# Routing stage of a two-layer kernel: key sums after the next chunk's second key tile, with keys kept in two buffers

## The reference, cut to what matters

```python
xn = _layernorm(x)
s = L1_attn(xn)          # linear attention
g = silu(L1_ffn(xn))     # 64 experts, top 6, and a shared expert
x = x + s * g

# of L1_attn, the part that the change touches
k = gelu(x @ Wk.T + bk) + 0.21
v = x @ Wv.T + bv
k_r = rope(k)
z = 1.0 / (einsum("bhnd,bhd->bhn", qh, kh.mean(axis=2)) + 1e-06)   # sum of k over a sequence
kv = einsum("bhnd,bhne->bhde", krh * scale, vh * scale)            # sum of k_r (x) v over a sequence
```

## Time and profile before

| what | value |
|---|---|
| time, median of 3 runs | 6141.93 us (6138.8 to 6146.82) |
| the profiled execution's own time | 6135.09 us |
| its span in the trace | 6133.2 us |
| busy share of the span | PE 85%, DVE 72%, ACT 46%, POOL 49% |
| granted TensorE clock, mean | 0.923 |

### The profile page before, as it was taken

The page is one execution under the profiler, slowest core; times in us unless marked ns, Lnnn a source line. Parts: engine busy times, 40 slices in busy tenths (PEclk is TensorE's granted clock), DMA queues, the critical chain, the costliest instruction groups (busy, mean ns, idle before and its releaser), DMA issues. The chain is left out here.

```text
span 6133.2 us, 79104 instructions
## 1 busy us (share of the span) xinstructions
PE 5235.2 (85%) x26286; PEld 3098.7 (51%) x26286; DVE 4390.5 (72%) x8723; ACT 2850.5 (46%) x6074; POOL 3005.0 (49%) x1603
## 2 busy tenths in 40 slices
PE   6777677676757999999899899999989988888877
PEld 2222222222214666666555566666655555556755
DVE  5999999999996777777333477777743347674249
ACT  5666666766653555555111255555521123332233
POOL 5989989989994444444111244444411100002724
PEclk8888888888868999999999999999999989999988
DMA  5555555554541111111211111111121143333655
GB/s 130 127 118 132 134 122 129 131 127 124 122 100 47 32 35 32 36 32 32 64 52 52 50 34 34 35 32 35 32 57 52 52 137 124 115 115 110 167 178 191
DMA packets 475672, 530.96 MB, mean 87 GB/s; under 512 B 56438, under 2 KB 377988, under 8 KB 471172
## 3 DMA queue, kind: packets, MB, share of 16 engines
q1 hardware_dynamic: 456132, 515.24, 30.9%
q10 hardware_dynamic: 6848, 8.67, 0.5%
q0 software_dynamic: 12288, 2.00, 0.3%
HBM read 395.83 MB, written 146.82 MB: 88 GB/s over the span
## 5 line engine op out<-in xcount | busy, mean ns | idle before, releaser
L607 POOL TENSOR_TENSOR db<-durep,brep 128x2048 f32<-128x2048 f32 x256 | 1160.6, 4534 | 165.9 <-DVE p_h L514 155.7
L1080 POOL TENSOR_TENSOR rn<-n,mhalf 128x16 f32<-128x16 f32 x128 | 374.9, 2929 | 1077.7 <-DVE n L1041 1077.7
L466 ACT ACTIVATE p_h<-dlrep,am 128x512 f32<-128x512 f32 x1024 | 704.1, 691 | 210.5 <-DVE hh L525 179.2
L321 PE MATMUL p_acc<-hh,fold 128*32 128x512 f32 x2048 | 351.1, 765 | 511.7 <-DVE hh L525 510.7
L514 DVE TENSOR_TENSOR_SCAN p_h<-p_h,hlast,db 128x512 f32<-128x512 f32 x576 | 717.4, 1276 | 0.0
L935 ACT ACTIVATE probT<-p_t 128x512 f32<-128x512 f32 x256 | 152.9, 597 | 817.0 <-PE p_t L852 817.0
L525 DVE TENSOR_TENSOR hh<-p_h,crep 128x512 f32<-128x512 f32 x768 | 515.0, 671 | 0.0
L797 PE MATMUL p_qk<-wqkv,hT 128*128 128x512 f32 x1024 | 485.9, 598 | 2.5 <-DVE rot_sin L1035 1.6
L1374 POOL TENSOR_TENSOR grstd<-grstd,mhalf 128x4 f32<-128x4 f32 x32 | 32.6, 1018 | 789.7 <-DVE grstd L1301 789.7
L865 PE MATMUL p_o<-probT,v 128*64 128x128 f32 x4096 | 405.7, 279 | 12.6 <-DVE probT L1018 7.3
L865 PEld LDWEIGHTS p_o<-probT,v 128*64 128x64 f32 x4096 | 343.9, 137 | 136.7 <-issue 98.1
(11 more groups left out here) (269 smaller groups left out, 11836.8 us busy)
## 6 DMA issues: line engine op xcount, KB each, us to landing
dlrep<-delta_rows SPq DMA_DIRECT2D x256, 256.0 KB
durep<-drive_rows SPq DMA_DIRECT2D x256, 256.0 KB
ew<-in_L_ffn_w SPq DMA_DIRECT2D x192, 176.0 KB
brep<-bc_rows SPq DMA_DIRECT2D x64, 256.0 KB
crep<-bc_rows SPq DMA_DIRECT2D x64, 256.0 KB
delta_rows<-dl SPq DMA_DIRECT2D x64, 256.0 KB
drive_rows<-du SPq DMA_DIRECT2D x64, 256.0 KB
hx<-stream SPq DMA_DIRECT2D x256, 64.0 KB
```

The costliest lines, as they stand in the source:

```text
L321: ins = pe.matmul(p_acc[32 * j:32 * j + 32, :], fold[:], hh[s % 2][:, j], start=False, stop=(g == NG - 1), skip_group_check=True)
L466: act.activation(p_h[:, (i % BANKS) * CH:(i % BANKS + 1) * CH], dlrep[use % 2][:, j], ACT.Exp, scale=am[:, q, j, g:g + 1]).then_inc(s_ex, 1)
L607: pool.tensor_tensor(out=db[s % 2][:], in0=durep[use % 2][:], in1=brep[c % 2][:, g:g + 1, :].to_broadcast([P, 4, CH]), op=ALU.mult).then_i ...
L1080: pool.tensor_tensor(out=rn[k][:], in0=n2[k][:], in1=mhalf[:], op=ALU.pow).then_inc(s_rn, 1)
```

## The change

TensorE's `key_sums(c - 1)` is moved from behind `gate_scores(c)` to behind `keys(c, 1)`. Since keys(c, 0) would now overwrite rks before the sums of chunk c - 1 have read it, rks gets a second buffer and chunks alternate between them. VectorE's wait for the sums in keys(c, 0) is for the chunk two before, and `rotate(c)`, which has still one tile kr, gets a wait for the sums of chunk c - 1. VectorE's reading of a finished batch is moved from behind shared(c, 0) to behind normalise(c + 1), since the bank is complete only then. No instruction of work is added or removed.

```diff
-    ks = sb("rks", [P, CT, 2 * D])
+    ks = [sb(f"rks{k}", [P, CT, 2 * D]) for k in range(2)]
...
-    kg, vg = ks[:, :, 0:D], ks[:, :, D:2 * D]
+
+    def kg(c):
+        return ks[c % 2][:, :, 0:D]
+
+    def vg(c):
+        return ks[c % 2][:, :, D:2 * D]
...
                 gate_scores(c)
-                if c > 0:
-                    key_sums(c - 1)
                 shared(c, 0)
                 keys(c, 0)
                 if c > 0:
                     invert(c - 1)
                 keys(c, 1)
+                if c > 0:
+                    key_sums(c - 1)
                 shared(c, 1)
...
             def keys(c, j):
-                if j == 0 and c > 0:
-                    dve.wait_ge(s_kvsum, c)
-                    dve.wait_ge(s_kr, c)
+                if j == 0 and c > 1:
+                    dve.wait_ge(s_kvsum, c - 1)
+                    dve.wait_ge(s_kr, c - 1)
...
             def rotate(c):
...
                 dve.wait_ge(s_kg, c + 1)
-                dve.scalar_tensor_tensor(out=kr[:], in0=kg, scalar=KB, in1=cs[:, u, :, 0], op0=ALU.add, op1=ALU.mult)
+                if c > 0:
+                    dve.wait_ge(s_kvsum, c)
+                    dve.wait_ge(s_kr, c)
+                dve.scalar_tensor_tensor(out=kr[:], in0=kg(c), scalar=KB, in1=cs[:, u, :, 0], op0=ALU.add, op1=ALU.mult)
...
                 shared(c, 0)
-                if c % CPB == 0 and c > 0:
-                    key_sums(c // CPB - 1)
                 keys(c, 0)
...
                     normalise(c + 1)
+                if c % CPB == 0 and c > 0:
+                    key_sums(c // CPB - 1)
                 shared(c, 1)
```

More of the change, by code:

```diff
@@ L1595, in key_sums @@
                 for j in range(CT):
-                    pe.matmul(p_ks, ones[:], kg[:, j], start=(u == 0 and j == 0), stop=False, skip_group_check=True)
+                    pe.matmul(p_ks, ones[:], kg(c)[:, j], start=(u == 0 and j == 0), stop=False, skip_group_check=True)
                 pe.wait_ge(s_kr, c + 1)
@@ L1600, in key_sums @@
                         fs = slice(f * P, (f + 1) * P)
-                        ins = pe.matmul(p_kv[:, fs], kr[:, j, fs], vg[:, j, fs], start=False,
+                        ins = pe.matmul(p_kv[:, fs], kr[:, j, fs], vg(c)[:, j, fs], start=False,
                                         stop=(u == CPB - 1 and j == CT - 1 and f == DH - 1), skip_group_check=True)
@@ L1669, in keys @@
                 act.wait_ge(s_ka, 4 * c + 4)
-                act.activation(kg, kg, ACT.Gelu).then_inc(s_kg, 1)
+                act.activation(kg(c), kg(c), ACT.Gelu).then_inc(s_kg, 1)
             def gate_scores(c):
@@ L1738, in keys @@
             def keys(c, j):
-                if j == 0 and c > 0:
-                    dve.wait_ge(s_kvsum, c)
-                    dve.wait_ge(s_kr, c)
+                if j == 0 and c > 1:
+                    dve.wait_ge(s_kvsum, c - 1)
+                    dve.wait_ge(s_kr, c - 1)
                 dve.wait_ge(s_kp, 4 * c + j + 1)
-                dve.tensor_tensor(out=ks[:, j], in0=p_k[j % 2][:], in1=b_kv[:], op=ALU.add).then_inc(s_ka, 1)
+                dve.tensor_tensor(out=ks[c % 2][:, j], in0=p_k[j % 2][:], in1=b_kv[:], op=ALU.add).then_inc(s_ka, 1)
             def rotate(c):
                 u = c % CPB
-                s2, i2, o2 = (v.rearrange("p j (h two) -> p j h two", two=2) for v in (kg, cs[:, u, :, 1], kt[:]))
+                s2, i2, o2 = (v.rearrange("p j (h two) -> p j h two", two=2) for v in (kg(c), cs[:, u, :, 1], kt[:]))
                 if c < CPB:
```

## The result

The changed kernel takes 6083.86 us (median of 4 runs, 6077.37 to 6085.71) against 6141.59 us (6138.8 to 6146.82) before: a ratio of 0.9903, 95% interval [0.9886, 0.992], or 57.7 us less. The profiled execution took 6085.71 us, with a span of 6083.8 us and a mean granted clock of 0.929.

The account below looks back on a forecast made before the run. In route, TensorE's wait for kr at a lowered clock lengthened lmx to second block; 15 such stretches fall from 188.4 to 130.4 us, the rest of the period unchanged. Gain 58 us, 6141.93 to 6084 us, range 6076 to 6101.

Parts of the forecast that it names:

- leg B: Part of route's chunk period from TensorE's start of the shared expert's second block to the next lmx: unchanged at 24.67 us.
- VectorE's side of leg A: VectorE's chain from lmx through macc and sh(c, 0) to TensorE's second block: 8.69 us, and it decides.
- leg A: Route's chunk period from lmx to TensorE's start of the second block: 12.87 us in chunk 7, becoming 8.69.
- the restart of TensorE: Between sh's end and the second block's matmul, weight load included: 0.30 us, as in chunk 0.
- the 0.04 us between macc and sh: On VectorE, an allowance of 0.04 us between the end of macc and the start of sh(c, 0).
- TensorE's side: From lmx, TensorE's wait for lsub, then invert, keys(c, 1), rotated and plain sums: through at 8.00 us, 0.69 before VectorE.
- The clock: TensorE in route keeps its upper clock through new waits of 1.98 and 0.69 us; chance 0.60.
- two waits of 1.70 and 1.73 us: TensorE's last two waits in the stage before, under 4 us between them, granted clock 1.00: the nearest evidence.
- The 1.98 us: TensorE's forecast wait ahead of invert, for lsub, counted from start to start.
- The change that does nothing: Rival: route is held by its transfers or ScalarE, gain within the noise, 6142 us; chance 0.04.
- all four groups at the lower clock: Rival: TensorE's 6.95 us between lsub and second block at half speed, through at 14.95, 6173 us; chance 0.02.
- The clock rival: The 1.98 us wait lowers the clock in some or all chunks, TensorE ends leg A, 6084 to 6099 us; chance 0.30.

Follow-up runs that it names:

- experiment 4: Changed kernel with matmuls added on TensorE behind each chunk's key sums: first kernel 0.43 us a chunk, 6082.08 us; second kernel 1.71 us, 6097.61 us.
- experiment 1: Kernel before with the two key buffers and changed waits alone, key sums and batch's read where they stood: 6143.04 us, ratio 1.0.
- experiment 6: Changed kernel with VectorE's sh(c, 0) inside choose(c), 6068.6 us; last kernel also key sums behind TensorE's third block, batch's read behind last keys, 6049.78 us.
- experiment 3: Changed kernel with the key sums one place earlier on TensorE, behind keys(c, 0) and before invert: 6100.0 us, ratio 0.9927.
- experiment 5: Changed kernel with one VectorE instruction of 128x1024 elements (1.22 us) added ahead of lmx in chunks 2 to 15: 6101.14 us, ratio 0.9935.

## Why the prediction was right

**What bounds, and leg B.** Right. The two legs changed as they were named: A fell, B stayed within 0.21 us, 0.15 in most chunks. Of this 0.11 us belongs to a small effect which I had put elsewhere: a block of matmuls that starts behind a wait is slower to get going. The second block and the positions behind it take 5270.08 - 5266.13 = 3.95 us, where they take 3.84 us in the second kernel of experiment 4, without a wait. The rest, 0.04 us and 0.10 in the first chunks, stands in experiment 1 too, where the order is the old one; what makes it was not tried. VectorE's read of the batch was rightly put at nothing: the legs of the chunks 4, 8 and 12, which have it, agree with those of the chunk behind each within 0.02 us. In the last kernel of experiment 6, where it stands elsewhere, it costs 0.66 us each time.

**VectorE's side of leg A.** Right in what decides, mis-sized by a third of a microsecond: 8.33 us instead of 8.69. The term is the restart of TensorE, "0.30 us" from chunk 0. It measured 0.06 us (sh ends at 5266.07, the matmul starts at 5266.13). In chunk 0 the matmul came 0.25 us behind its weight load; why it does not here was not tried. And the 0.04 us between macc and sh was -0.09: sh starts at 5265.39, before the end of macc's row at 5265.48. Over the chunks 1 to 14 this is 14 x 0.36 = 5.0 us that the forecast did not have.

**TensorE's side.** Right: it comes second, and its sum was 8.00 us where 7.57 us were measured from start to start when nothing held it (experiment 6). The plain sums, 1.73 us instead of 1.95, the start of invert, 0.94 instead of 1.05, and the rotated sums, 1.79 instead of 1.89, make the difference. Experiments 3 and 4 show the slack from both sides: less of it gains nothing in leg A, 0.43 us more is hidden, 1.71 us more costs 0.96. Chunk 15 is the exception that I left out when I took 15 times 8.69. No mix stands in chunk 14's list, so lmx comes 3.3 us sooner, TensorE is not yet at invert, and leg A is 8.97 us there.

**The clock.** Right, and now measured. The forecast leaned on two waits of 1.70 and 1.73 us; the real waits are 1.69 (at most 1.76) and 0.60 us, and the granted clock is 1.00 from chunk 1 on. The 1.98 us that I compared with them was counted from start to start, and they by their rows; counted like it, the real wait is 5258.74 - 5255.17 - 1.72 = 1.85 us. So the new wait was as long as the two known ones, and not a quarter of a microsecond longer, as the rival had it. By the Trainium skill, "TensorE: Matmul & The Clock Gate", section "A second HAM failure mode: psum-queue depth-cycling", frequent short pauses between groups of matmuls make the clock go up and down. The changed kernel does not agree, with two pauses in each chunk and a clock of 1.00 for 490 us. In experiment 3 the clock did go down and up, but with one pause of 2.4 to 2.5 us a chunk; whether this is the case that the page describes, no run here shows.

**The size.** 58 us forecast, 57.7 measured. That it fits this well is luck: leg A gave 62.9 us instead of 58, leg B took 2.2 back and chunk 0, by chance, 1.6, which leaves the 59.1 us of the stage in the two profiles; the medians, with the scatter of the rest of the program, have 1.4 us less.

**The rivals.** The change that does nothing and all four groups at the lower clock are out by the result itself, with a period of 33.15 us and a clock of 1.00; experiment 5 adds that even where the clock does fall, leg A ends at 9.3 us at the latest, not at 14.95. (The price of that second rival was also too low: 15 x 14.95 less 188.4 is 36 us, not 31.) The clock rival was not met by the change, but experiments 3 and 5 show that it was near: with a wait of 2.4 or 2.8 us instead of 1.7, the clock falls in some of the chunks.

## What to carry to other kernels

Cut the period of a loop at the instruction where two engines meet, and give each side of each leg its own sum; what a move is worth is then the difference of two sides, and the side that will decide next is known before the run. A wait of TensorE costs twice if it is long enough to bring the clock down, as the wait of 4.3 us did, which took 2.6 us more by the clock; two waits of 1.7 and 0.6 us took nothing more. Where work that fills gaps can be placed freely, make the longest gap that remains short, rather than close one gap wholly. When the freed engine has slack left, look for the same kind of move on the other engine: the earlier place of VectorE's sh and the later one of the key sums brought another 34 us.

## What the runs showed of the hardware that I had not expected

How long TensorE may idle before its clock falls showed no sharp edge. In this stage a wait of 1.67 to 1.76 us with 0.60 us after it never brought it down (14 chunks of the changed kernel), one of 2.42 to 2.51 us did it in 8 chunks of 14 (experiment 3), one of 2.81 to 3.15 us in 3 of 13 (experiment 5), and one of 4.27 to 4.29 us in each of the chunks 1 to 14 of the kernel before. The longer of the two middle waits did it less often, and within one kernel waits of the same length went both ways: 2.44 us in the chunks 7 and 8 of experiment 3, 2.81 us in the chunks 7 and 9 of experiment 5, each with the clock down in the first only. So the length alone does not tell; what else decides was not tried. A fall cost 1.6 to 1.7 us in experiment 3, where it lay in leg B, and 0.5 to 0.9 us in experiment 5, where TensorE's slack in leg A took up a part.

A block of eight matmuls behind a short wait, at the upper clock, took 0.11 us longer than one behind none, though its first matmul started 0.06 us after the release.
